# Final sum of the last expert layer: the scaling goes from VectorE to ScalarE, the adds are joined three tiles at a time, and every fourth tile goes to GpSimd

## What is computed

```python
routing_weights, selected = phi_routing(logits)
wte = zeros((T, E)).at[arange(T)[:, None], selected].add(routing_weights)
for e in range(E):
    h = silu(x @ w1[e].T) * (x @ w3[e].T)
    out = out + wte[:, e:e + 1] * (h @ w2[e].T)
...
x = x + out
```

## Time and profile before

| | |
|---|---|
| time, median of 3 runs | 1807.62 us (1802.72 to 1809.69) |
| span of the profiled execution | 1839.1 us |
| mean granted TensorE clock, share of full speed | 0.897 |
| TensorE busy | 1491.7 us, 81% of the span |
| VectorE, ScalarE, GpSimd busy | 1062.8, 901.8, 943.4 us |
| last scatter issued by GpSimd | 1815.07 us |
| the 32 operations of the final sum on VectorE | 1823.30 to 1836.06 us |
| end | 1839.1 us |

### The profile page before, as it was taken

The page is one execution under the profiler, slowest core; times in us unless marked ns, Lnnn a source line. Parts: engine busy times, 40 slices in busy tenths (PEclk is TensorE's granted clock), DMA queues, the critical chain, the costliest instruction groups (busy, mean ns, idle before and its releaser), DMA issues. The chain is left out here.

```text
span 1839.1 us, 29734 instructions
## 1 busy us (share of the span) xinstructions
PE 1491.7 (81%) x10638; PEld 1231.6 (67%) x10638; DVE 1062.8 (58%) x2174; ACT 901.8 (49%) x1610; POOL 943.4 (51%) x742
## 2 busy tenths in 40 slices
PE   5887888899968768944299997985885999899984
PEld 2566666678746668923168887972774788788873
DVE  6777879689768653456744554457746323233223
ACT  5897797999645534624132234534442322232221
POOL 0599798899738627810011236020624429582771
PEclk8899999899988969976589999988886999899987
DMA  3001010101030075340000000030043503242144
GB/s 130 24 25 47 24 44 28 47 38 55 1 107 2 2 243 181 118 142 17 2 0 1 1 1 1 1 88 7 1 159 142 142 3 116 81 144 75 52 139 163
DMA packets 54577, 119.21 MB, mean 65 GB/s; under 512 B 14448, under 2 KB 35443, under 8 KB 46884
## 3 DMA queue, kind: packets, MB, share of 16 engines
q1 hardware_dynamic: 45556, 84.38, 13.3%
q0 software_dynamic: 8448, 32.91, 5.5%
q10 hardware_dynamic: 432, 0.03, 0.0%
HBM read 92.78 MB, written 24.43 MB: 64 GB/s over the span
## 5 line engine op out<-in xcount | busy, mean ns | idle before, releaser
L878 POOL TENSOR_TENSOR HC<-H,CB 128x512 f32<-128x512 f32 x256 | 321.7, 1287 | 77.1 <-DVE H L786 63.2
L604 ACT ACTIVATE UT<-DTXT,BT 128x512 f32<-128x512 f32 x256 | 181.5, 711 | 28.2 <-PE ps L452 27.8
L452 PE MATMUL ps<-ident,UT 128*128 128x128 f32 x1024 | 166.8, 289 | 28.5 <-DVE H L786 16.6
L452 PEld LDWEIGHTS ps<-ident,UT 128*128 128x128 f32 x1024 | 124.3, 147 | 89.7 <-DVE H L786 40.6
L614 ACT ACTIVATE dA<-DT,nA 128x512 f32<-128x512 f32 x256 | 181.3, 710 | 3.4 <-DVE H L786 3.3
L786 DVE TENSOR_TENSOR_SCAN H<-dA,ps 128x512 f32<-128x512 f32 x128 | 152.3, 1212 | 45.1 <-PE ps L452 36.8
L786 DVE TENSOR_TENSOR_SCAN H<-dA,HL,ps 128x512 f32<-128x512 f32 x128 | 157.5, 1269 | 25.7 <-PE ps L452 17.6
L461 PE MATMUL ps<-ident,HC 128*128 128x128 f32 x1024 | 158.1, 282 | 11.2 <-POOL HC L878 9.2
L2317 DVE TENSOR_TENSOR f_XN<-f_XN,ps 128x1024 f32<-128x1024 f32 x39 | 47.6, 1222 | 178.1 <-PE ps L160 150.2
L158 PE MATMUL ps<-f_W,f_DIT 128*128 x312 | 130.1, 417 | 10.3 <-POOL f_W L2023 7.1
L461 PEld LDWEIGHTS ps<-ident,HC 128*128 128x128 f32 x1024 | 123.0, 146 | 19.1 <-POOL HC L878 18.7
(11 more groups left out here) (558 smaller groups left out, 4159.0 us busy)
## 6 DMA issues: line engine op xcount, KB each, us to landing
CB<-m_c_rows SPq DMA_DIRECT2D x16, 1024.0 KB
f_w<-in_f_w SPq DMA_DIRECT2D x16, 1024.0 KB, 5.2
f_stage<-in_f_w POOLq DMA_DIRECT2D x15, 1024.0 KB, 5.2
f_stage<-in_f_w SPq DMA_DIRECT2D x9, 1024.0 KB, 4.9
f_xn_rows<-f_XN SPq DMA_DIRECT2D x8, 512.0 KB, 12.0
f_W<-f_y_rows SPq DMA_DIRECT2D x4, 1024.0 KB, 9.2
f_rows_in<-f_DI SPq DMA_DIRECT2D x23, 128.0 KB
f_DI<-f_rows_in SPq DMA_DIRECT2D x23, 128.0 KB, 2.3
```

The source lines that it names most:

```text
L452: ins = pe.transpose(PS[4 + G % UR][:, t * P:(t + 1) * P], UT[:, n % 2, t, c * P:(c + 1) * P], g.ident[:, :])
L604: act.activation(UT[:, N % 2, t, :], DTXT[:, k % 2, t, :], ACT.Copy, scale=BT[:, k % 2, t, n:n + 1]).then_inc(ut_ready, 1)
L878: pool.tensor_tensor(HC[:, y, :], H[:, s, :], CB[:, n // 4 % CR, n % 4, :], ALU.mult).then_inc(hc_ready, 1)
```

## The change

ScalarE scales: in each group it multiplies the six expert rows of the first three tiles by their gates, in place in `GR`, and the first expert's row of the fourth tile too, seven operations of 128x256. VectorE adds: two operations per group, each on three tiles at once (128x768), one for each expert. GpSimd takes the fourth tile: it scales the second expert's row, adds the first (which ScalarE has scaled), then adds its own. The store of a group waits for both of VectorE's adds and both of GpSimd's. A new semaphore tells ScalarE and GpSimd that the gates are there. The loads, the stores and their order are as before, and so is everything ahead of the final sum.

```diff
@@ SyncE
-                    sp.wait_ge(added, 8 * (j + 1))
+                    sp.wait_ge(added, 2 * (j + 1))
+                    sp.wait_ge(added_last, 2 * (j + 1))
                     sp.dma_start(g.out[:, 4 * j:4 * j + 4, :], g.X[:, 4 * j:4 * j + 4, :]).then_inc(out_stored, 16)
@@ GpSimd, behind the last scatter
+                pool.wait_ge(gates_ready, 1)
+                for j in range(NT // 4):
+                    t = 4 * j + 3
+                    pool.wait_ge(gathered[j], 16)
+                    pool.tensor_scalar(GR[:, t, 1, :], GR[:, t, 1, :], mult2[:, t:t + 1], None, ALU.mult).then_inc(scaled_last, 1)
+                    pool.wait_ge(scaled_first, j + 1)
+                    pool.tensor_tensor(g.X[:, t, :], g.X[:, t, :], GR[:, t, 0, :], ALU.add).then_inc(added_last, 1)
+                    pool.wait_ge(added_last, 2 * j + 1)
+                    pool.wait_ge(scaled_last, j + 1)
+                    pool.tensor_tensor(g.X[:, t, :], g.X[:, t, :], GR[:, t, 1, :], ALU.add).then_inc(added_last, 1)
@@ ScalarE, behind the last block
+                act.wait_ge(gates_ready, 1)
+                for j in range(NT // 4):
+                    act.wait_ge(gathered[j], 16)
+                    for q, m in enumerate((mult1, mult2)):
+                        for t in range(4 * j, 4 * j + 3):
+                            act.activation(GR[:, t, q, :], GR[:, t, q, :], ACT.Copy, scale=m[:, t:t + 1]).then_inc(scaled, 1)
+                        if q == 0:
+                            t = 4 * j + 3
+                            act.activation(GR[:, t, 0, :], GR[:, t, 0, :], ACT.Copy, scale=m[:, t:t + 1]).then_inc(scaled_first, 1)
@@ VectorE
                     if k == 2:
                         weight(m2[:, :], v3(OH1), mult2[:, :], 1)
+                        dve.sem_inc(gates_ready, 1)
                 for j in range(NT // 4):
-                    dve.wait_ge(gathered[j], 16)
-                    for q, m in enumerate((mult1, mult2)):
-                        for t in range(4 * j, 4 * j + 4):
-                            if q:
-                                dve.wait_ge(added, 8 * j + t % 4 + 1)
-                            dve.scalar_tensor_tensor(g.X[:, t, :], GR[:, t, q, :], m[:, t:t + 1], g.X[:, t, :], ALU.mult,
-                                                     ALU.add).then_inc(added, 1)
+                    ts = slice(4 * j, 4 * j + 3)
+                    for q in range(2):
+                        dve.wait_ge(scaled, 6 * j + 3 * (q + 1))
+                        if q:
+                            dve.wait_ge(added, 2 * j + 1)
+                        dve.tensor_tensor(g.X[:, ts, :], g.X[:, ts, :], GR[:, ts, q, :], ALU.add).then_inc(added, 1)
```

More of the change, by code:

```diff
@@ L1936, in ffn1 @@
         added, room_free, out_stored = sem("added"), sem("room_free"), sem("out_stored")
+        scaled, scaled_first, scaled_last = sem("scaled"), sem("scaled_first"), sem("scaled_last")
+        added_last, gates_ready = sem("added_last"), sem("gates_ready")
         WPARTS = ("f1_w1", "f1_w3", "f1_w2")
```

## The result

The changed kernel takes 1816.51 us (median of 4 runs, 1816.43 to 1822.09), the kernel before 1808.19 us in the same comparison (1802.72 to 1809.69). The ratio is 1.0052, with a 95% interval of 1.0036 to 1.0068: slower by some 8 us where 2.5 were forecast, and outside the stated range of 1804.5 to 1815.

A forecast was written before the change was run, and what follows sets the result against it. Gather landings and VectorE's final sum were taken to bound the end; GpSimd, at 3.6 us per group after 1827.8, would end at 1838.6 against 1836.1, +2.5 us on 1807.6: 1810.1 us, range 1804.5 to 1815.

The forecast's parts named there:

- What bounds the kernel, and the room: Final sum: gathers land every 2.7 us with DMA engines full, so the change can win only one or two microseconds.
- 0.40 us per start: ScalarE's scaling operations of 128x256 in the final sum start 0.40 us apart, one taking 0.50 us; 2.8 us per group.
- rival 2: Final sum: ScalarE's operations do not overlap at 256 columns, 0.50 us per start, +2.2 us; chance 0.1.
- VectorE's add: Final sum: each VectorE add of 128x768 takes 0.96 us, of which 0.80 is the pass over the columns.
- GpSimd's multiply: Final sum: GpSimd's scaling of one 128x256 row takes 0.8 us, taken between the ends 0.41 and 1.24.
- The increment in block 2: VectorE's new semaphore increment makes it wait for its reciprocal; counted as nothing, under 0.3 us if uncovered.
- The wait between GpSimd and VectorE: Final sum: the later operation waits for the earlier one's pass, 0.21 us of each VectorE pass hidden; 3.6 us per group.
- The upper bound, +5.1: Final sum with GpSimd's multiply at 1.24 us and nothing of VectorE's passes hidden: 1812.7 us.
- nothing is queued behind their new waits but the end of the program: Program end: ScalarE and GpSimd, idle before the sum, hold up no later work by waiting; no cost was counted.
- Rival 1: Final sum: ScalarE sets the pace, the other engines' operations fit in gaps; -0.5 us, 1807.1 us; chance 0.15.
- 4 (the floor): Final sum: the last group ends as soon as the gathered data allow; -0.7 us, 1806.9 us; chance 0.05.
- Rival 3: Final sum: slower by over 0.5%, GpSimd's operations doubled beside the gathers' transfers, 6.1 us per group; +10 us, 1818; chance 0.04.

The follow-up runs named there:

- sems: The kernel before with the five new semaphores and VectorE's increment behind the gates, final sum as before: 1808.68 us, ratio 1.0003.
- base: The kernel before, unchanged, run and profiled again: 1808.76 us, ratio 0.9998.
- no_vec: The changed kernel with all waits kept, VectorE's adds cut to one column per tile: 1814.52 us, ratio 1.0039 to the kernel before.
- changed: The changed kernel, unchanged, run and profiled again: 1817.97 us, ratio 1.0042 to the kernel before.
- late_pe: The kernel before, with TensorE waiting for VectorE's 32nd operation of the final sum and then doing one transpose: 1808.28 us, ratio 1.0002.
- scal_vec: The changed kernel without GpSimd's part: ScalarE scales all eight rows per group, VectorE adds four tiles at a time; 1810.07 us, ratio 1.0006 to the kernel before.

## Why the prediction was wrong

- **What bounds the kernel, and the room.** Right: the gathers still land 2.7 us apart (after, 5.6 to 12.1 us behind their issue; in all runs the first 5.2 to 5.7 and the last 11.9 to 12.5), and ScalarE starts with the first. The best version found wins 1.0 us of the room of one or two.
- **ScalarE**, 0.40 us per start and 0.50 for one: measured 0.49, seven operations in 2.79 us. Right; rival 2 is out.
- **VectorE's add**, 0.96 us: measured 0.96, and up to 1.16 where GpSimd was first.
- **GpSimd's multiply**, 0.8 between 0.41 and 1.24: measured 0.93. Its adds 0.72, and 0.80 apart, as from the rows.
- **The increment in block 2**, under 0.3 us: VectorE's next operation starts 0.40 us behind the start of the reciprocal in the run sems and 0.28 in base, so it costs 0.12 us. Right to count it as nothing.
- **The wait between GpSimd and VectorE.** Right as a mechanism, and shown by no_vec. Its size was wrong in terms that cancelled. I let 0.21 us of each of VectorE's passes hide between GpSimd's operations; here nothing hides. With the measured multiply the group is 0.93 + 1.64 + 2 x 0.80 = 4.2 us, and measured it is 4.2 (multiplies at 1795.98, 1800.16 and 1804.35 in the run changed). The 0.21 came from rows with another order: there a subtraction of VectorE starts 0.4 us behind an add of GpSimd (1132.83 behind 1132.45), and it is VectorE's that grows, by 0.28 us. The trace of the changed kernel has the whole pass instead: an add of GpSimd that starts 0.03 us behind VectorE's takes 1.52 us in place of 0.72, longer by the 0.80 that I had worked out for the pass. That the two second adds stand for one interface, as the sum has it, no run shows; the timeline shows VectorE's at 1798.45 with its usual 0.96 us and GpSimd's over at 1800.0, 1.55 us for both where I had 0.96 + 0.6. The upper bound, +5.1, has 1.3 us for "nothing hidden" (six times 0.21, my estimate); the second and third groups came out that way, 4.2 us each against 3.6. Against that, the last group has VectorE's work already behind it and takes 2.4 us, not 3.6. The first group took 4.5 us, as forecast; for the other three 3 x 3.6 us were forecast and 4.2 + 4.2 + 2.4 measured, both 10.8. That the 15.2 us for the sum, +2.5, was hit is luck in this part. VectorE keeps step with ScalarE and is held up in only two of its eight adds, by 0.2 us (1.16 and 1.15), so that its last two adds fall into GpSimd's third group, not its fourth.
- **The step that failed** is the sentence "nothing is queued behind their new waits but the end of the program", and with it "the last store is 512 KB as before, 2.6 us behind it". I took the end of the program to cost what it did before, and a late GpSimd nothing. The trace of before had shown GpSimd's last scatter issued 24 us ahead of the span's end, and that is cover; I did not ask what the end would cost with the cover gone. It is 9.5 us from GpSimd's last instruction to the end, of which 2.6 lie under the last store's landing and a few tenths under the hand-overs: 6.7 us.
- **The rivals.** Rival 1 (ScalarE sets the pace) and 4 (the floor) are out. Rival 3 had the right side and even the size, +10, but by another mechanism: a GpSimd slowed by the transfers did not arise, since in no_vec all its operations are short beside them (0.93 and 0.72 us), and its group took 4.2 us, not 5.8. With 0.04 on it I had the case of over 0.5% far too low, for want of a mechanism at the program's end.

The sum as it should have been: +2.5 in the final sum and +6.5 to 6.7 at the end make +9.0 to 9.2 us, 1817; measured 1816.5 and 1818.0. The mechanism was half right: the final sum came as forecast, partly by luck, and the larger part of the loss was not in the forecast at all.

## What to carry to other kernels

An engine that is idle at the end of a program may need time of its own to get from its last instruction to the end (GpSimd here: 9.5 us), hidden because its stream ends early. Before giving it late work, hold it there with nothing but a wait and time that: one line showed here two thirds of the loss (0.29% of 0.42%). And where VectorE and GpSimd wait for each other's passes, add the passes of both when you size a group: 2.5 us of GpSimd's own work became 4.2 beside VectorE's.

## What the runs showed of the hardware

- From the last instruction of GpSimd's stream to the end of the program it is 9.5 us in this program, in four kernels (from 1796.5, 1803.3, 1804.7 and 1806.8 to the end), whether GpSimd cleared two columns or added; with a wait alone the program ends 9.7 us behind the add that it waits for. For the others no such time shows: the program ends 2.5 us behind TensorE's last operation (late_pe), 3.0 behind VectorE's (base) and 4.3 behind ScalarE's (scal_vec). Why it is so long was not tried, and stays open; the indirect DMAs that GpSimd issues in this kernel may or may not have to do with it. Not every meeting of the engines has it. Behind the short block at the very start of the run base, ahead of any DMA that GpSimd issues, GpSimd stops at 2.0 and the first stage begins at 3.4, 1.4 us later (the number in brackets in the second row). At all later changes of stage in that trace GpSimd had been idle for at least 10.5 us (632.9 to 643.4 is the shortest), so they can't tell.

```profile
1.72 0.28 POOL L229 TENSOR_SCALAR_AFFINE_SELECT upper<-ones 128x128 f32<-128x128 f32 x1
...
3.44 0.53 POOL L880 MEMSET XP<- 128x512 f32 x1 [1.44 <-POOLq L186]
```

- The view of waits names TensorE's sequencer for it, and a late TensorE costs nothing (late_pe, ratio 1.0002, wait 0.2 us): the name behind a wait at this barrier was not the cause of it.
- In the changed kernel a GpSimd operation that starts behind one of VectorE's is longer by about what is left of VectorE's pass (estimated at 0.80 us for 768 columns, from the 1.04 ns a column of the prediction). Behind an add of 768 columns an add of 0.72 us became 1.52 when it started 0.03 us later, and 1.21 when it started 0.34 us later. The multiply, which reads one tensor from SBUF, is held too: 0.93 became 1.63, 0.33 us behind an add of VectorE that itself took 1.16.
- GpSimd's multiply of 128x256 by one value per partition takes 0.93 us, longer than its add of two tensors (0.72), both in no_vec.
